# A selective-scan kernel: the product dt times x of the high channels is made by VectorE in the forward bodies, by GpSimd in the backward ones

## What is computed

```
xr  = silu(conv(x @ W_in))                       # 192 channels
dbl = xr @ W_xproj                               # gives dt's rank-6 part, B and C
dt  = softplus(dbl[..., :6] @ W_dt + b_dt)
h   = exp(dt * A) * h + (dt * x) * B             # 192 x 16 states, one step per pixel
y   = sum over states of h * C
```

## Time and profile before

| | us |
|---|---|
| median of 3 runs | 5826.39 |
| lowest, highest | 5824.25, 5832.24 |
| the profiled execution | 5823.86 |
| its span | 5822.1 |

### The profile page before, as it was taken

One profiled execution on the slowest core, in us unless ns is written; L12 is line 12 of the kernel. 1 busy time (PEld: TensorE's weight loads), 2 busy tenths in 40 slices (PEclk: granted clock), 3 DMA queues, 4 the chain that ended last, 5 costly groups with the idle time before them and its releaser, 6 DMA issues.

```text
span 5822.1 us, 66909 instructions
## 1 busy us (share of the span) xinstructions
PE 4627.1 (79%) x13259; PEld 1367.2 (23%) x13259; DVE 5275.9 (91%) x4497; ACT 4528.6 (78%) x6861; POOL 5157.2 (89%) x2128
## 2 busy tenths in 40 slices
PE   8877887778877788777887788777887778877887
PEld 3222222222222222222222222222222222222222
DVE  2499999999999999899999999999999999999998
ACT  3588778787878877787877877878777878788786
POOL 0299999999999989999999999999999999899998
PEclk8887888878887888887887888887888888888888
DMA  4377767767767677677677677677776776776776
GB/s 109 83 169 172 171 164 170 174 160 176 176 163 174 161 173 173 159 172 170 163 170 170 164 172 169 163 173 164 170 175 164 168 176 160 173 173 161 170 174 153
DMA packets 419916, 959.63 MB, mean 165 GB/s; under 512 B 56944, under 2 KB 57193, under 8 KB 384984
## 3 DMA queue, kind: packets, MB, share of 16 engines
q1 hardware_dynamic: 419544, 955.73, 69.1%
HBM read 771.41 MB, written 184.11 MB: 164 GB/s over the span
## 4 chain that ended last, share of the span: by engine, by line
DVE 23%; issue 21%; PE 19%; DMA 14%; ACT 12%; POOL 5%; SPq 3%; DVEq 1%; ACTq 1%; POOLq 0%
DVE X L1386 15%; DMA bc_d<-bc 6%; DVE X L1370 5%; PE ps L783 4%; ACT ps L1105 3%; POOL X L1492 3%; PE ps L762 3%; DMA xp<-in_x 3%; PE ps L708 3%; PE ps L817 2%; DVE hid L1350 2%; PE ps L788 2%; DMA lo_d<-bc 2%; SPq L541 1%; DMA lo<-lo_d 1%
## 5 line engine op out<-in xcount | busy, mean ns | idle before, releaser
L1492 POOL TENSOR_TENSOR X<-X,cR 128x2048 f32<-128x2048 f32 x768 | 3478.2, 4529 | 61.8 <-POOL carry L1490 0.2
L1386 DVE TENSOR_TENSOR_SCAN X<-ps,carry,X 128x512 f32<-128x512 f32 x2688 | 3264.8, 1262 | 156.0 <-ACT ps L1105 134.1
L1105 ACT ACTIVATE ps<-hi,amat 128x512 f32<-128x512 f32 x2048 | 1374.6, 682 | 659.0 <-DVE X L1386 655.8
L1482 POOL TENSOR_TENSOR X<-lo,bR 128x2048 f32<-128x2048 f32 x258 | 1168.0, 4527 | 36.5 <-DMA lo<-lo_d 35.5
L1370 DVE TENSOR_TENSOR X<-hi,ps 128x2048 f32<-128x2048 f32 x512 | 1159.1, 2264 | 11.2 <-PE ps L817 9.9
L817 PE MATMUL ps<-X,red 128*32 128x512 f32 x6144 | 896.2, 663 | 330.4 <-POOL X L1492 328.8
L783 PE MATMUL ps<-win,w_u 97*128 97x512 f32 (+1 forms) x2080 | 1106.3, 681 | 1.8 <-ACT xr L1060 0.9
L1105 ACT ACTIVATE ps<-lo,amat 128x512 f32<-128x512 f32 x1026 | 687.0, 677 | 132.4 <-DVE X L1386 90.7
L798 PE MATMUL ps<-xr,wd 128*96 128x512 f32 (+1 forms) x520 | 458.0, 979 | 321.9 <-ACT xr L1060 272.6
L708 PE MATMUL ps<-xp,w 96*128 96x512 f32 x768 | 493.6, 775 | 103.4 <-DMA xp<-in_x 102.0
L783 PEld LDWEIGHTS ps<-win,w_u 97*128 97x128 f32 (+1 forms) x2080 | 372.0, 189 | 658.6 <-issue 644.7
(11 more groups left out here) (125 smaller groups left out, 4124.9 us busy)
## 6 DMA issues: line engine op xcount, KB each, us to landing
hi<-hi_d SPq DMA_DIRECT2D x516, 512.0 KB, 8.4
bR<-bc_d SPq DMA_DIRECT2D x516, 256.0 KB, 4.5
cR<-bc_d SPq DMA_DIRECT2D x516, 256.0 KB, 7.2
lo<-lo_d SPq DMA_DIRECT2D x516, 256.0 KB, 4.7
hi_d<-S SPq DMA_DIRECT2D x258, 256.0 KB, 8.1
y_d<-yf SPq DMA_DIRECT2D x128, 256.0 KB, 9.6
yb<-y_d SPq DMA_DIRECT2D x112, 256.0 KB, 9.0
win<-xn_d SPq DMA_DIRECT2D x130, 196.3 KB
```

Source lines behind the costliest of these rows:

```text
L1105: A_(p_a[i % RING][:, :], dt, ACT.Exp, scale=amat[:, column(i):column(i) + 1]).then_inc(s_exp, 1)
L1386: V.tensor_tensor_scan(h, a, h, 0.0 if head else carry[:, i:i + 1], ALU.mult, ALU.add).then_inc(s_scan, 1)
L1482: G.tensor_tensor(batch(par, s), lo[:, LOW:2 * LOW, :].unsqueeze(1).to_broadcast([P, 2, 2, CH]), quads(bR, par, s), ALU.mult).then_inc(s_b ...
L1492: G.tensor_tensor(batch(par, s), batch(par, s), quads(cR, par, s), ALU.mult).then_inc(s_hc, 1)
```

## The change

In forward bodies VectorE multiplies dt by x right behind `make_dt(0)`, ahead of the scan of tile 6; GpSimd's `times_x(0)` is left out there. Backward bodies and the prologue are as before. The new function waits for the same semaphore that GpSimd's waited for, now set by VectorE's own previous instruction, and gives the same signal.

```
+            def times_x_high(u, b, par):
+                bank, at = u.at["D0"]
+                dve.wait_ge(s_pf[bank], at + 2)
+                V.tensor_tensor(S[:, 1, :], S[:, 0, :], xr[0][:, par, :], ALU.mult).then_inc(s_dtx[0], 1)
...
                     if i == 6:
                         make_dt(0, u, n + 1)
+                        if not rev:
+                            times_x_high(u, n + 1, nxt)
...
                 times_c(n, 0, par, rev)
-                times_x(0, u, nxt)
+                if rev:
+                    times_x(0, u, nxt)
                 times_c(n, 1, par, rev)
```

## The result

The changed kernel took 5881.8 us in the median (5867.2 to 5892.6, 4 runs), beside 5825.3 us of the kernel before on the same chip. The ratio is 1.0097, with a 95% interval of 1.0081 to 1.0113: slower by 0.97%, or 56 us. The forecast was 5975 us, slower by 2.6%. The sign was right and so was the mechanism of the wait; how often the long wait occurs was not, and the size was 2.7 times too large (151 us against 56). The profiled execution of the changed kernel took 5867.2 us, the lowest of its runs, so its trace shows 43 of the 56 us.

A forecast was written before the change was run, and what follows sets the result against it. In forward bodies VectorE and GpSimd were taken as equally loaded, VectorE setting the period. Own work 47 plus meeting 184 minus 80 hidden gave +151 us on 5823.9, 5975 us (+2.6%); own range 5910 to 6050, for 8 in 10 5795 to 6050.

The forecast's parts named there:

- The upper end for the meeting: VectorE's new product waits until the GpSimd instruction under way is over: 3.1 us in one body, 0.3 in another.
- the two ends: Bounds on the new product's wait beside GpSimd in forward bodies: 0, or until GpSimd's instruction under way is over.
- Which pattern holds: Whether VectorE's product meets GpSimd's product with C (3.1 us) or the end of `times_x(1)` (0.3 us) in forward bodies.
- the first pattern: GpSimd's product with C is under way when VectorE's product is ready; claimed for 57 forward bodies at 3.1 us.
- Its own work: The added product on VectorE: 0.73 us more per forward body, 47 us over 64.
- The lump of 80 us: The part of VectorE's lateness taken to vanish in its forward-body waits for TensorE and ScalarE: 80 us subtracted.
- The relief: `times_x(0)` gone from GpSimd in forward bodies: 1.27 us each, 81 us of its queue in 64 bodies.
- the first rival: No meeting in forward bodies, and GpSimd's relief shortens VectorE's waits: -29 us, 5795 us, -0.5%; chance 0.19.
- the second rival: No meeting in forward bodies, but the relief is worth less: about 0, 5824 us, within the noise; chance 0.08.
- the third rival: The meeting exists but GpSimd stays behind, 20 bodies at 3.2 us, 44 at 0.6: +78 us, 5902 us; chance 0.09.
- the balance: Forward loads after the change, GpSimd 39.2 us and VectorE 40.9 a body, so GpSimd catches up 1.7 us each body.
- Backward bodies and SyncE's stores: Claimed to cost nothing: backward bodies keep order and load, and `store_high` is issued after the new product ends.

The follow-up runs named there:

- The cut tail: The changed kernel with GpSimd's product with C of batch 5 covering two of four tiles in forward bodies: 5949 us, ratio 1.0248 against the kernel before.
- The variant without a meeting: The changed kernel with VectorE's added product reading its first operand from the dt projection's PSUM bank: ratio 1.0009 against the kernel before, 5 us.

## Why the prediction was right or wrong, point by point

- **The upper end for the meeting: right.** The wait for the whole instruction holds: the product lasts 3.66 us in the body shown, 3.0 of them waiting, where 3.1 was taken from the earlier trace rows; the twelve long ones wait 3.1 us on average. The trace of before could not show it. The Trainium skill ("SBUF — State Buffer", section "SBUF: two separate sides") stated it, and these runs agree (0.68 us with one operand in PSUM, up to 4.93 with both in SBUF), for forward and backward bodies and for either engine as the one that waits. No row of before decided between the two ends: that the prediction took this one was, as it says, a choice.
- **Which pattern holds: wrong, and this is the step that failed.** "After the first body or so of each forward run the first pattern must hold", 57 bodies at 3.1 us and 7 at 1, made 184 us. Measured: 12 bodies with a product of over 3 us, most others with a wait of 0.0 to 0.6, 56 us in all. The step compared the loads of a whole body, 39.2 against 40.9 us, and let GpSimd gain 1.7 us a body. But GpSimd can't carry a gain over: before the product with C of batch 2 it waits for the scan of tile 11 (2.10 us at 1857.66 above), and there everything won earlier in the body is given back. By the traces it waited there (over 0.2 us) in 57 of the 64 forward bodies already before the change, 74 us in all, and in all 64 after it, 128 us. From that point on only the rest counts. In the body after 1800.03 GpSimd passes that wait at 1816.28 and reaches its next low product at 1844.20, 27.9 us later, while VectorE needs 24.7 us to its next low dt sum (1841.02, 3.2 us ahead of it). So GpSimd comes about 3 us late to the meeting in every body without a disturbance (3.1 in the median of the 64), whatever is taken off it before tile 11. The cut tail shows this: 2.2 us less *behind* that point, and 53 of 64 products wait for the long one.

  The twelve long meetings are exactly the bodies in which its low product starts only 0.7 to 2.0 us behind the low dt sum, against 2.2 to 4.4 in the other 52. One is the first body of the program; ahead of the other eleven VectorE was held up, in six of them (each the third body of a forward run) by a pause of 2.7 to 5.1 us.
- **Its own work and what hides: the cost was right, the hiding went with the wrong wait.** Where the product takes 0.69 us, the next instruction starts 1.30 us after `make_dt(0)` (0.58 before): 0.72 us more a body, where the prediction had 0.73 and 47 us in all. So the 0.12 us for a linked pair, which it kept against the rule it cites, hold too. The lump of 80 us was for a wait of 184. Own work and waits added 47 + 56 = 103 us, and 56 show, so 47 are hidden; with the wait put right and the 80 left as it was, the sum would have been +23. In the tail-cut kernel, which has the 184 us, 47 + 184 = 231 us show as 144, so 87 are hidden, close to the 80. The more VectorE is late, the more of its waits go: its idle time in forward bodies is 158 us in the trace before, 107 in the changed kernel and 66 with the tail cut. Where the meeting is taken away, the own work alone shows as 5 us (0.9996 to 1.0022).
- **The relief: rightly left out of the forecast's sum, wrong in the first rival.** The rival without a meeting let GpSimd's relief shorten VectorE's waits for TensorE by 50 us, to 5795 us. VectorE's waits for TensorE did shrink, but leaving the product out gained nothing (1.0004). The variant without a meeting is that rival run on the chip, and it came out even: the second rival, "within the noise".
- **The nearest of the cases was the third rival**, GpSimd stays behind, at +78 us and with a chance of 0.09. It used the counts of the trace as they stood; the balance spoken of against it was the error. It overstated the long meetings, 20 in place of 12, and by them the waits, 91 us in place of 56.
- **Backward bodies and SyncE's stores: unchanged, as said.** `store_high` is issued at least 6.8 us behind the end of the product in all 64 forward bodies of the trace after.

## What to carry to other kernels

The VectorE product with two SBUF inputs that was measured here costs what GpSimd happens to be doing at that moment. Price such an instruction by the neighbour's position, not by its own duration. Place it where GpSimd waits for a later scan of VectorE's own: in the backward bodies none of the 64 met anything there, in the forward ones 9 met the end of a GpSimd product that was not yet done. Or give it an operand in PSUM, where the sum allows it. To say where an engine will stand in a loop, don't compare the loads of a whole pass: find the last point in the pass at which it waits for the other, and count both engines' work from there. Work taken off ahead of such a point is lost in it; work taken off behind it moves the engine, and may move it into a collision.

## What the runs showed of the hardware that was not expected

- The wait for the other engine is not in the idle time of the records but inside the duration: 692 to 4925 ns for one instruction with the same shape. A group's mean (1562 ns) hides that it is two populations, 52 under 2 us and 12 over 3.
- GpSimd is held up in turn when VectorE was first: a copy of four columns took 0.64 us in place of 0.19, a product of 512 columns 1.71 in place of 1.27. Those copies end 0.04 us behind VectorE's product.
- Less work on GpSimd made the changed kernel slower by 1.5%, from 1.0097 to 1.0248, and in the kernel before the same cut did nothing (0.9995).
